# One stationary operand for both heads of a pair in the first score pass, and a prologue in another order

## The chip, the cores and the metric

The kernel runs on one core of a Trainium2 chip. Times are device microseconds of one execution; the profile is of one execution, taken by the hardware profiler. The engines are TensorE (PE in the rows; PEld is its weight load), VectorE (DVE), ScalarE (ACT), GpSimd (POOL) and SyncE (SP), which issues most DMA transfers. Each runs its own instructions in order and waits on semaphores.

## The reference

One layer of a language model tower on 32 sequences of 512 tokens, D = 256, all in float32. Cut to what matters:

```python
h = (tok_table[x] + pos_table + seg_table[seg]) * sqrt(256)      # seg: a running maximum over x == 102
xn = layernorm(h)
Q, K, V = heads(xn @ wq), heads(xn @ wk), heads(xn @ wv)         # 16 heads of 16
sc = einsum('bhnid,bhnjd->bhnij', Qb, Kw) / 4                    # a block of 64 queries, 128 keys: its own block and the one before
local = softmax(where(mask, sc, -inf)) @ Vw
GQ = heads(xn @ wgq)                                             # 8 latent heads of 16
GK, GV = heads(chunk_means(xn @ wgk)), heads(chunk_means(xn @ wgv))   # 64 latents
rem = softmax(where(lmask, GQ @ GK.T / 4, -inf)) @ GV @ r_out_w
h = h + (sigmoid(gate_l(Q)) * local + sigmoid(gate_r(Q)) * rem) @ w_out
h = h + ffn(layernorm(h))      # 8 experts, each takes the 2048 tokens that score best for it
```

## The kernel before

The program has a prologue, a loop over 32 sequences (written out, not a loop on the chip), and the experts. In the loop a sequence has five score passes, s = 0 to 4: s = 0 the latents, s = 1 to 4 the four tiles of 128 queries. A softmax needs the maximum of each row before its exponential, so every pass is made twice. The first pass (`top_scores`) puts queries on the partitions of the four PSUM banks `banks`; VectorE takes row maxima (`dve_tops`, L1160, into `mx`, or `mxl` for the latents). TensorE transposes these (task `MX`, L781), ScalarE negates and copies them (`low`, `lowl`), and SP writes them as extra rows into the query tiles by DMA (`Qt<-low` L467, `Gq<-lowl` L463). The second pass (`key_scores`) puts keys on the partitions and streams the queries: the extra row of Q times a row of ones in K takes the maximum off, and ScalarE's exponential (L686) follows. `values` (L1059, L1065) multiplies the probabilities with V. The second pass of u = s - 1 follows the first pass of s, and `half(2s)` stands between them.

Heads lie in pairs: 32 partitions (a strip, g = 0 to 3) hold two heads of 16. Two copies of each tensor exist, j = 0 and 1: `Qt[par][:, j, ...]` and `Kt[par][:, j, ...]` hold head j of the pair, with zeros in the other head's 16 rows, but for the row 16 * (1 - j) of each strip: it is the extra row of Q, and ones in K. ScalarE writes copies, zeros and ones in one go out of PSUM, by a scale per partition (`c_query`, `c_parity`) and a bias per partition (`c_unit`). In the first pass Q's extra row is still zero. Each score matmul uses one 32x64 tile of the array; eight tiles (four strips, two halves a) can be at work at a time. A float32 matmul is two records in the trace, so L1003 has 32 matmuls and 64 records in a pass. Ahead of them 16 bf16 records (L995) add the mask.

`plan` is a table written by hand: ten halves of tasks per sequence (projections Q, K, G, PK, PV, V and transposes ET for the next sequence; RT, RO, MT, WO for the output of a tile). Each engine walks through it in the same order. SP's `store` walks through it too: the rows of maxima after MX, and after WO the finished tile to `h_rows` (L474), which waits for GpSimd's factors (`s_fac`).

The prologue loads all weights and tables (SP, L449; everything waits for `s_load`, all 20 loads), turns token ids into rows of indices (VectorE L1332 to L1338, TensorE's transposes L928 and L930, `idx_now` L1129), gathers embedding rows (GpSimd L510), adds position and segment (VectorE `dve_embed`, L1136 on), normalises (GpSimd `pool_norm`, L517 to L525) and projects the first sequence (`head_tasks`, L776 on, Q at L802).

Of the kernel before, what the change touches and what calls it, by code (L numbers as in the profile page):

```python
# [26 lines left out]
P = 128  # L27
D = 256
# [30 lines left out]
def constants(S):  # L59
# [6 lines left out]
    unit = np.stack([i % 32 == HD, i % 32 == 0], 1)  # L66
# [19 lines left out]
    cols = [f(ident), f(parity * HD ** -0.5), f(parity), f(parity * (NL / S)), f(unit), f(before), f(lane), f(i),  # L86
# [6 lines left out]
def tower(nc, ins, out, cin, din, widths, SEQS, S, V, F, E):  # L93
# [12 lines left out]
    with ctx:  # L106
# [23 lines left out]
        (c_ident, c_query, c_parity, c_latent, c_unit, c_before, c_lane, c_part, onehot, ownhot, by_query, even_key, odd_key,  # L130
# [108 lines left out]
        r2 = sba("r2", [P, H, HD])  # L239
        mix = sba("mix", [P, D])  # L240
# [16 lines left out]

        s_load = sem("s_load")
# [166 lines left out]
        LOADS = 20  # L425
# [4 lines left out]
        def _(sp):  # L430
# [3 lines left out]
                (xi[:, :], ins["x"]), (cst[:, :], cin), (digits[:, :, :].rearrange("p a b -> p (a b)"), din),  # L434
                (b1_rows[:, :], ins["b1"].rearrange("e (m p) -> (e m) p", p=P)),
                (segs[:, 0, :], ins["seg_table"][0:1, :].to_broadcast([P, D])),
                (segs[:, 1, :], ins["seg_table"][1:2, :].to_broadcast([P, D])),
                (P16[:, :, :], ins["pos_table"].rearrange("(t p) d -> p t d", p=P)),
                (wq[:, :, :], v2(ins["wq"])), (wk[:, :, :], v2(ins["wk"])),
                (wvg[:, :, 0:D], v2(ins["wv"])), (wgq[:, :, :], v2(ins["wgq"])),  # L440
                (wgk[:, :, :], v2(ins["wgk"])), (wgv[:, :, :], v2(ins["wgv"])),
                (wro[:, :], ins["r_out_w"]), (wout[:, :, 0:D], v2(ins["w_out"])),
                (gates[:, 0, :], ins["gate_local_w"].rearrange("(a h) d -> a (h d)", a=1).to_broadcast([P, D])),
                (gates[:, 1, :], ins["gate_remote_w"].rearrange("(a h) d -> a (h d)", a=1).to_broadcast([P, D])),
                (cen[:, :], ins["centroids"]),
                (ln_rows[0:KC, :], v1(ins["ln_g"])), (ln_rows[KC:2 * KC, :], v1(ins["ln_b"])),
# [143 lines left out]
        def _(pool):  # L590
# [42 lines left out]
        def act_misc(act, m, task, b, nx):  # L633
# [20 lines left out]
            elif name == "Q":  # L654

                for j in range(2):
                    ins_ = nc.scalar.activation(Qt[nx][:, j, t, :], bank[:, :], ACT.Copy, scale=c_query[:, j:j + 1])
                ins_.then_inc(s_mA, 1)
            elif name == "K":

                for j in range(2):
                    ins_ = nc.scalar.activation(Kt[nx][:, j, t, W:], bank[:, :], ACT.Identity,
                                                scale=c_parity[:, j:j + 1], bias=c_unit[:, j:j + 1])
                ins_.then_inc(s_mA, 1)
            elif name == "G":
                for j in range(2):
                    ins_ = nc.scalar.activation(Gq[nx][:, j, :], bank[:, :], ACT.Copy, scale=c_query[:, j:j + 1])
                ins_.then_inc(s_mA, 1)
            elif name == "PK":
                for j in range(2):  # L670
                    ins_ = nc.scalar.activation(Gk[nx][:, j, :], bank[:, 0:NL], ACT.Identity,
                                                scale=c_latent[:, j:j + 1], bias=c_unit[:, j:j + 1])
# [56 lines left out]
        def _(act):  # L729

            act.wait_ge(s_init, 3)
# [191 lines left out]
        def _(pe):  # L923
            pe.wait_ge(s_load, 16 * LOADS)
            pe.wait_ge(s_init, 3)

            for t in range(TS):
                nc.tensor.transpose(M_ps[0][:, t * SEQS:(t + 1) * SEQS], xw[:, t * P:(t + 1) * P],  # L928
                                    c_ident[0:SEQS, 0:SEQS])
                nc.tensor.transpose(M_ps[0][:, (TS + t) * SEQS:(TS + t + 1) * SEQS], xs[:, t * P:(t + 1) * P],  # L930
                                    c_ident[0:SEQS, 0:SEQS])
            for c in range(KC):
                mm = nc.tensor.transpose(M_ps[1][:, c * E:(c + 1) * E], cen[:, c * P:(c + 1) * P], c_ident[0:E, 0:E])
# [545 lines left out]
```

## Time and profile before

| | |
|---|---|
| three runs | 2906.99, 2922.24, 2924.91 us; median 2922.24 |
| the profiled execution | 2924.72 us; its span 2922.7 us |
| busy in the span | PE 2667.8 us (91%), DVE 1737.8 (59%), ACT 1233.5 (42%), POOL 967.7 (33%) |
| TensorE's mean granted clock | 0.963 |

The span is what the profiler saw from the first to the last instruction; the 2 us to the time of the execution lie around it. A share of busy time is a mean over three stages of different kind, so the rows further down are read by stage.

### The profile page before, as it was taken

To read this page: it belongs to the slowest core of one execution; us is meant where nothing else is said; L and a number is where in the kernel's file an instruction comes from. 1 tells how busy PE (TensorE), PEld (TensorE's weight loads), DVE (VectorE), ACT (ScalarE), POOL (GpSimd) and SP (SyncE) were. 2 spreads that over 40 slices of the span, in tenths; PEclk is the share of its full clock that TensorE was granted. 3 is DMA by queue.
4 is the path that set the end of the run, shared out by engine and by line. 5 is a ranking of instruction groups with operands and counts; after the bars stand their busy time and mean duration, and the time that the engine had idled before them with its cause. 6 is when DMAs were issued, how large, how long until landed. Compare 5 with 4: busy or idle time off the path is not lost. (4 is left out here: it accounts for less than half of the span.)

```text
span 2922.7 us, 109244 instructions
## 1 busy us (share of the span) xinstructions
PE 2667.8 (91%) x47656; PEld 1862.1 (64%) x47656; DVE 1737.8 (59%) x5573; ACT 1233.5 (42%) x2659; POOL 967.7 (33%) x1417
## 2 busy tenths in 40 slices
PE   2799999999999999999999997169999999999998
PEld 1566677767767767677676676136666666666665
DVE  3466666666656666566665654766667575675700
ACT  0444444544444445454444542034434334344342
POOL 2323323323323324233233220024353443434433
PEclk9899999999999999999999998579999999999999
DMA  2000001000000000000000000101121112211120
GB/s 65 19 22 24 24 22 26 25 24 23 24 24 23 24 24 26 22 24 24 23 26 22 24 19 14 35 26 40 57 69 32 66 32 69 66 37 64 33 69 28
DMA packets 58915, 98.31 MB, mean 34 GB/s; under 512 B 12124, under 2 KB 43816, under 8 KB 58440
## 3 DMA queue, kind: packets, MB, share of 16 engines
q0 software_dynamic: 18624, 51.14, 6.2%
q1 hardware_dynamic: 39816, 40.17, 4.2%
q8 instruction: 378, 6.19, 0.9%
q14 instruction: 97, 0.79, 0.1%
HBM read 55.88 MB, written 33.82 MB: 31 GB/s over the span
## 5 line engine op out<-in xcount | busy, mean ns | idle before, releaser
L895 PE MATMUL banks<-hT,w 128*128 128x512 f32 x1024 | 468.6, 605 | 11.0 <-ACT hT L712 10.9
L1160 DVE TENSOR_REDUCE mx<-banks 128x8 f32<-128x1024 f32 x256 | 301.3, 1219 | 150.5 <-PE banks L1003 150.5
L686 ACT ACTIVATE probT<-banks 128x1024 f32<-128x1024 f32 x256 | 259.8, 1028 | 231.9 <-PE banks L1046 231.9
L723 ACT ACTIVATE hid<-banks,b 128x512 f32<-128x512 f32 x256 | 176.3, 689 | 399.0 <-PE banks L895 399.0
L532 POOL TENSOR_TENSOR h<-ve,mhalf 128x2 f32<-128x2 f32 x128 | 92.0, 719 | 737.1 <-DVE ve L1201 737.1
L895 PEld LDWEIGHTS banks<-hT,w 128*128 128x128 f32 x1024 | 187.6, 192 | 213.0 <-issue 197.3
L510 POOL DMA_INDIRECT rows<-in_tok_table,idx_now x132 | 138.5, 1049 | 475.3 <-DVE hres L1138 390.1
L1059 PEld LDWEIGHTS V_ps<-Ve,probT 128*64 128x64 f32 x4096 | 257.7, 141 | 34.4 <-issue 34.2
L1059 PE MATMUL V_ps<-Ve,probT 128*64 128x17 f32 x4096 | 271.4, 213 | 4.9 <-issue 4.9
L1059 PE MATMUL V_ps<-Vo,probT 128*64 128x17 f32 x4096 | 271.8, 213 | 2.2 <-issue 2.2
L1235 DVE TENSOR_SCALAR_CACHE_REDUCE hits<-act_s,cval 128x128 bf16<-128x128 f32 x960 | 261.2, 343 | 2.3
L1059 PEld LDWEIGHTS V_ps<-Vo,probT 128*64 128x64 f32 x4096 | 257.8, 141 | 4.1 <-issue 4.0
L575 POOL TENSOR_TENSOR orow<-orow,b 128x256 f32<-128x256 f32 x128 | 133.5, 1043 | 368.6 <-DVE orow L1325 367.5
L908 PE MATMUL M_ps<-w,hid 128*128 128x256 f32 x1024 | 231.6, 379 | 0.0
L908 PE MATMUL V_ps<-w,hid 128*128 128x256 f32 x1024 | 231.5, 379 | 0.0
L908 PEld LDWEIGHTS V_ps<-w,hid 128*128 128x128 f32 x1024 | 192.7, 190 | 38.9 <-issue 15.3
L908 PEld LDWEIGHTS M_ps<-w,hid 128*128 128x128 f32 x1024 | 190.3, 190 | 23.6
L1040 PE MATMUL banks<-Qt,Kt 32*64 32x128 f32 x4096 | 190.3, 284 | 3.1 <-issue 3.1
L1181 DVE TENSOR_TENSOR r<-M_ps,sg 128x256 f32<-128x256 f32 x128 | 54.4, 425 | 231.4 <-PE M_ps L787 230.3
L1040 PEld LDWEIGHTS banks<-Qt,Kt 32*64 32x64 f32 x4096 | 166.4, 132 | 23.0 <-issue 4.0
L1046 PE MATMUL banks<-Qt,Kt 32*64 32x64 f32 x4096 | 173.9, 225 | 7.5 <-issue 7.4
L1042 PE MATMUL banks<-Qt,Kt 32*64 32x64 f32 x4096 | 178.0, 228 | 0.5 <-issue 0.5
(223 smaller groups left out, 5566.2 us busy)
## 6 DMA issues: line engine op xcount, KB each, us to landing
h_rows<-h SPq DMA_DIRECT2D x128, 130.0 KB, 2.0
w<-in_w SPq DMA_DIRECT2D x16, 1024.0 KB, 5.3
Qt<-low SPq DMA_DIRECT2D x512, 2.0 KB
Gq<-lowl SPq DMA_DIRECT2D x256, 2.0 KB
rows<-in_tok_table,idx_now POOLq DMA_INDIRECT x132, 3.5
out_rows<-orow,idx_cur POOLq DMA_INDIRECT x128, 2.5
b<-in_b SPq DMA_DIRECT2D x8, 128.0 KB, 4.5
hrow<-h_rows,idx_next POOLq DMA_INDIRECT x64, 2.8
```

The lines of the kernel that those rows point to most:

```text
L510: nc.gpsimd.indirect_dma_start(rows[:, t, :], None, ins["tok_table"], bass.IndirectOffsetOnAxis(idx_now[:, t:t + 1], 0)).then_inc(s_rows[t ...
L575: nc.gpsimd.tensor_tensor(out=orow[:, q % 2, :], in0=orow[:, q % 2, :], in1=b2[:, :], op=ALU.add).then_inc(s_add, 1)
L686: nc.scalar.activation(dst[:, 2 * pair:2 * pair + 2, :], banks[:, 2 * pair:2 * pair + 2, :], ACT.Exp).then_inc(s_exp, 1)
L723: nc.scalar.activation(hid[:, m, :], S_ps[m % 2][:, 0:GT * P], ACT.Gelu_apprx_tanh, bias=b1[:, m:m + 1]).then_inc(s_hid, 1)
L895: mm = nc.tensor.matmul(S_ps[m % 2][:, 0:GT * P], w1[:, c, m * P:(m + 1) * P], hT[g % 2][:, c, :], start=c == 0, stop=c == KC - 1)
L908: mm = nc.tensor.matmul(O_ps[q % 2][:, 0:D], hid[:, m, q * P:(q + 1) * P], w2[:, m, :], start=m == 0, stop=m == FC - 1)
L1040: nc.tensor.matmul(banks[side[0], g, n * P:(n + 1) * P], k[:, W + at_:P + at_], q[:, at_:at_ + P], start=False, stop=n == G - 1)
L1042: nc.tensor.matmul(banks[side[1], g, n * P:n * P + W], k[:, at_:W + at_], q[:, at_:at_ + W], start=False, stop=False)
L1046: mm = nc.tensor.matmul(banks[side[1], g, n * P + W:(n + 1) * P], k[:, P + at_:P + W + at_], q[:, at_ + W:at_ + P], start=False, stop=n == ...
L1059: nc.tensor.matmul(V_ps[side[a], h * OW:(h + 1) * OW], probT[t % 2][:, g, n * P + a * W:n * P + (a + 1) * W], vals[:, t, h, :], start=True ...
L1160: nc.vector.tensor_reduce(tops.rearrange("p (g h) -> p g h", g=2), banks[:, 2 * pair:2 * pair + 2, :].rearrange("p g (h k) -> p g h k", h= ...
L1235: ins_ = nc.vector.tensor_scalar(hits[:, c, :], act_s[:, :], cval[:, c:c + 1].bitcast(F32), None, ALU.is_ge, ALU.add, accum_out=counts[:, ...
```

## The change

- First pass: ScalarE no longer zeroes the other head's rows of Q (the scale is a constant), only those of K, and writes no ones. One stationary tile, `Qt[par][strip, 0, ...]`, now serves both heads: the moving operand is `Kt[par][strip, :, ...]`, both copies j side by side, 2 x 128 columns (latents: 2 x 64), and the output goes to two places of the bank. There are half as many matmuls, each twice as wide. Masks, second pass and values stay.
- A row of ones in K would now spoil the first pass, since Q has the other head's values there. So K's row is zero in the first pass, and SP writes the ones from a constant tile `units` by DMA, after the first pass that last reads these columns (`s_S`) and before the second pass that needs them, which waits for them on `s_low[u]` together with the maxima.
- Prologue: ids and the identity are loaded first on semaphores of their own; the other loads stand in another order; VectorE starts on the ids alone, and the sums for the gates and some of the set-up stand later; TensorE makes the transposes of indices ahead of the wait for all loads; GpSimd normalises sequence 0 ahead of the gathers for sequence 1, and sequence 1 ahead of those for 2.

```diff
--- before.py
+++ after.py
@@ block.sync @@
-                (xi[:, :], ins["x"]), (cst[:, :], cin), (digits[:, :, :].rearrange("p a b -> p (a b)"), din),
...
+                (cst[:, P:], cin[:, P:]), (digits[:, :, :].rearrange("p a b -> p (a b)"), din),
             ]
+            sp.dma_start(xi[:, :], ins["x"]).then_inc(s_x, 16)
+            sp.dma_start(cst[:, 0:P], cin[:, 0:P]).then_inc(s_ident, 16)
...
             def store(b, q):
                 m = Misc(b, q % 2)
-                for half in plan:
+                for n, half in enumerate(plan):
+                    if m.new and n % 2 == 0:
+                        scored = n // 2
+                        done = [0] if scored == 0 else [] if scored == 1 else [scored - 1, scored][:1 + (scored == NU - 1)]
+                        if done:
+
+                            sp.wait_ge(s_S, 2 * (NU * b + scored + 1))
+                        for u in done:
+                            for j in range(2):
+                                if u == 0:
+                                    sp.dma_start(Gk[q % 2][HD * (1 - j)::32, j, :], units[:, 0, 0:NL]).then_inc(s_low[u], 16)
+                                else:
+                                    sp.dma_start(Kt[q % 2][HD * (1 - j)::32, j, :, W + (u - 1) * P:W + u * P],
+                                                 units[:, :, :]).then_inc(s_low[u], 16)
...
@@ block.gpsimd @@
             for t in range(TS):
+                pool_norm(pool, 0, t, 0, None)
+            for t in range(TS):
                 pool_gather_rows(pool, 1, t)
             for t in range(TS):
-                pool_norm(pool, 0, t, 0, None)
+                pool_norm(pool, 1, t, 1, Misc("head"))
             for t in range(TS):
                 pool_gather_rows(pool, 2, t)
-            for t in range(TS):
-                pool_norm(pool, 1, t, 1, Misc("head"))
@@ act_misc @@
-                    ins_ = nc.scalar.activation(Qt[nx][:, j, t, :], bank[:, :], ACT.Copy, scale=c_query[:, j:j + 1])
+                    ins_ = nc.scalar.activation(Qt[nx][:, j, t, :], bank[:, :], ACT.Copy, scale=HD ** -0.5)
...
-                    ins_ = nc.scalar.activation(Kt[nx][:, j, t, W:], bank[:, :], ACT.Identity,
-                                                scale=c_parity[:, j:j + 1], bias=c_unit[:, j:j + 1])
+                    ins_ = nc.scalar.activation(Kt[nx][:, j, t, W:], bank[:, :], ACT.Copy, scale=c_parity[:, j:j + 1])
...
@@ block.tensor @@
+            pe.wait_ge(s_ident, 16)
+            pe.wait_ge(s_init, 1)
+            for t in range(TS):
+                nc.tensor.transpose(V_ps[:, t * SEQS:(t + 1) * SEQS], xw[:, t * P:(t + 1) * P],
+                                    c_ident[0:SEQS, 0:SEQS])
...
+            mm.then_inc(s_setT, 1)
+
             pe.wait_ge(s_load, 16 * LOADS)
...
@@ top_scores @@
-                    for n in range(2 * TS):
-                        j, t = divmod(n, TS)
+                    for t in range(TS):
...
-                                mm = nc.tensor.matmul(banks[side[a], g, n * NL:(n + 1) * NL],
-                                                      Gq[par][strip[g], j, at_:at_ + W], Gk[par][strip[g], j, :],
-                                                      start=False, stop=n == 2 * TS - 1)
...
+                                mm = nc.tensor.matmul(
+                                    banks[side[a], g, :].rearrange("p (j t n) -> p j t n", j=2, t=TS)[:, :, t, :],
+                                    Gq[par][strip[g], 0, at_:at_ + W], Gk[par][strip[g], :, :],
+                                    start=False, stop=t == TS - 1)
...
-                for n in range(G):
-                    j, c = divmod(n, KC)
+                for c in range(KC):
...
-                            mm = nc.tensor.matmul(banks[side[a], g, n * P:(n + 1) * P],
-                                                  Qt[par][strip[g], j, c, at_:at_ + W],
-                                                  Kt[par][strip[g], j, c, at_:at_ + P], start=False, stop=n == G - 1)
...
+                            mm = nc.tensor.matmul(
+                                banks[side[a], g, :].rearrange("p (j c k) -> p j c k", j=2, c=KC)[:, :, c, :],
+                                Qt[par][strip[g], 0, c, at_:at_ + W],
+                                Kt[par][strip[g], :, c, at_:at_ + P], start=False, stop=c == KC - 1)
@@ key_scores @@
-                pe.wait_ge(s_low[u], (16 * 2 * (TS if u == 0 else KC)) * (b + 1))
+                pe.wait_ge(s_low[u], 16 * 2 * (1 + (TS if u == 0 else KC)) * (b + 1))
@@ block.vector @@
-            dve.wait_ge(s_load, 16 * LOADS)
+            dve.wait_ge(s_x, 16)
...
+            dve.wait_ge(s_setT, 1)
+            nc.vector.tensor_copy(idx_all[:, :, 0:SEQS], V_ps[:, 0:TS * SEQS].rearrange("p (t b) -> p t b", t=TS))
...
+            dve_indices(dve, 0)
...
+            dve.wait_ge(s_load, 16 * LOADS)
             chain(dve, nc.vector.tensor_tensor(P16[:, :, :], P16[:, :, :],
...
+            m = Misc("head")
+            dve_indices(dve, 1)
+            dve_embed(dve, 0, 0, 0, 0)
+            dve.wait_ge(s_setT, 2)
...
+            dve_latents(dve, m, 0)
+            dve_indices(dve, 2)
             for t in range(TS):
-                dve_embed(dve, 0, t, 0, 0)
...
+                dve_embed(dve, 1, t, 1, 0)
             for task in head_tasks:
                 dve_misc(dve, m, task, None, 1, 0)
-            for t in range(TS):
-                dve_embed(dve, 1, t, 1, 0)
```

On TensorE, in the first sequence, the latent pass and the first pass of tile 0, before:

```order
L976 MATMUL banks<-cst 64x512 x8
L985 MATMUL banks<-Gk,Gq 64x64 x64
L776 MATMUL M_ps<-cst,xn 128x128 x8
L781 MATMUL M_ps<-cst,mxl 32x128
L802 MATMUL M_ps<-x1T,wq 128x512 x2
L995 MATMUL banks<-cst 64x512 x16
L1003 MATMUL banks<-Kt,Qt 64x128 x32
L781 MATMUL M_ps<-cst,mx 16x128
```

And after:

```order
L996 MATMUL banks<-cst 64x512 x8
L1004 MATMUL banks<-Gk,Gq 64x2x64 x32
L792 MATMUL M_ps<-cst,xn 128x128 x8
L797 MATMUL M_ps<-cst,mxl 32x128
L818 MATMUL M_ps<-x1T,wq 128x512 x2
L1015 MATMUL banks<-cst 64x512 x16
L1022 MATMUL banks<-Kt,Qt 64x2x128 x16
L797 MATMUL M_ps<-cst,mx 16x128
```

Nothing moved here; the two groups of score matmuls have half the count and twice the columns.

On SP, one sequence of even number in the loop, from its latent maxima on (low0 and low1 hold the maxima of two tiles in turn), before:

```order
L463 DMA Gq0<-lowl 4x128 x8
L474 DMA h1_rows<-h1 128x260
L467 DMA Qt0<-low0 4x128 x4
L474 DMA h1_rows<-h1 128x260
L467 DMA Qt0<-low1 4x128 x4
L474 DMA h1_rows<-h1 128x260
L467 DMA Qt0<-low0 4x128 x4
L467 DMA Qt0<-low1 4x128 x4
L474 DMA h1_rows<-h1 128x260
```

And after:

```order
L469 DMA Gk0<-units 4x64 x2
L481 DMA Gq0<-lowl 4x128 x8
L492 DMA h1_rows<-h1 128x260
L485 DMA Qt0<-low0 4x128 x4
L492 DMA h1_rows<-h1 128x260
L471 DMA Kt0<-units 4x2x128 x2
L485 DMA Qt0<-low1 4x128 x4
L492 DMA h1_rows<-h1 128x260
L471 DMA Kt0<-units 4x2x128 x2
L485 DMA Qt0<-low0 4x128 x4
L471 DMA Kt0<-units 4x2x128 x4
L485 DMA Qt0<-low1 4x128 x4
```

The transfers of ones stand ahead of the maxima of s = 0, 2, 3 and 4, each group behind a wait for that first pass; the pair of u = 2 is the second `Kt0<-units` group.

On VectorE, in the prologue, the way from the ids to the first embedding, before (from the sum of position and segment on):

```order
L1352 TENSOR_TENSOR P<-P,segs 128x1024
...
L1363 MEMSET mx 128x32
L1365 CAST idx_all<-M_ps 128x4x32
L1368 CAST idx_all<-M_ps 128x4x3
L1369 MEMSET seg_all 128x4x3
...
L1129 COPY idx_now<-idx_all 128x4
L1396 TENSOR_TENSOR cenT<-cenT,banks 128x16
L1398 COPY gprod<-banks 128x2x256
```

And after:

```order
L1370 MEMSET seg_all 128x4x3
L1373 CAST idx_all<-V_ps 128x4x32
L1376 CAST idx_all<-V_ps 128x4x3
L1149 COPY idx_now<-idx_all 128x4
L1378 COPY seg_all<-V_ps 128x4x32
L1381 MEMSET Ve 128x1360
...
L1389 MEMSET h 128x2
L1392 TENSOR_TENSOR P<-P,segs 128x1024
```

The copy into `idx_now`, which lets GpSimd gather, stood behind the sums of tables and gates; now it stands ahead of them and of the large memsets.

## Rows read from the trace of the kernel before

**Rows 1.** Two stretches: PE, PEld, DVE, ACT, POOL busy us (instructions), granted clock, DMA.

```profile
0.00:96.56 96.56, 31.23 (x230) 18.81 (x230) 34.13 (x108) 16.76 (x42) 27.55 (x41) 0.95 0.20 55
96.56:1796.00 1699.44, 1637.34 (x42277) 1180.48 (x42277) 1043.09 (x2588) 804.25 (x1831) 537.34 (x976) 0.98 0.09 23
```

**Rows 2.** TensorE's waits from 96.56 to 1796 us: total us, times, longest.

```profile
PE banks L985 <- issue: 16.4, 12, 2.1
...
PE V_ps L1059 <- issue: 7.2, 12, 0.9
...
PE M_ps L791 <- issue: 3.5, 2, 1.9
```

**Rows 3.** The queue that brings instructions: packets, MB, share of 16 engines.

```profile
q8 instruction: 378, 6.19, 0.9%
```

**Rows 4.** TensorE's timeline at three score passes: start us, duration us, group.

```profile
910.08 1.15 PE L1003 MATMUL banks<-Kt,Qt 32*64 32x128 f32 x64
911.17 0.33 PE L791 MATMUL M_ps<-cst,mix 128*128 128x128 f32 x1
...
915.65 1.04 PE L1029 MATMUL banks<-Gq,Gk 32*64 32x512 f32 x16
916.62 0.33 PE L784 MATMUL M_ps<-cst,rem 128*128 128x128 f32 x1
...
951.10 1.54 PE L985 MATMUL banks<-Gk,Gq 32*64 32x64 f32 x128
952.57 0.44 PE L791 MATMUL M_ps<-cst,mix 128*128 128x128 f32 x2
```

**Rows 5.** Timelines of SP, VectorE and TensorE around the first pass of s = 3.

```profile
915.59 2.13 SPq L467 DMA_DIRECT2D Qt<-low  x4
...
927.62 0.32 SPq L474 DMA_DIRECT2D h_rows<-h  x1
...
931.81 2.36 DVE L1160 TENSOR_REDUCE mx<-banks 128x8 f32<-128x1024 f32 x2 [3.68 <-PE banks L1003]
...
934.51 0.65 PE L1023 MATMUL banks<-cst 32*64 32x512 bf16 x16
```

**Rows 6.** DMA issues: count, KB each, median us from issue to landing.

```profile
h_rows<-h SPq DMA_DIRECT2D x128, 130.0 KB, 2.0
...
rows<-in_tok_table,idx_now POOLq DMA_INDIRECT x132, 3.5
```

**Rows 7.** Timeline of the prologue and of the first sequence, several engines.

```profile
0.73 0.40 SPq L449 DMA_DIRECT2D xi<-in_x  x1
...
15.86 0.41 DVE L1332 CAST xf<-xi 32x512 f32<-32x512 int32 x1 [15.86 <-DMA ln_rows<-in_ln_b]
...
18.37 1.21 DVE L1338 TENSOR_TENSOR_SCAN xs<-xf 32x512 f32<-32x512 f32 x1
...
35.92 0.17 DVE L1129 COPY idx_now<-idx_all 128x4 int32<-128x4 int32 x1
...
45.02 0.17 DVE L1128 COPY seg_now<-seg_all 128x4 f32<-128x4 f32 x1 [6.46 <-DMA rows<-in_tok_table,idx_now]
...
53.97 0.60 POOL L517 TENSOR_TENSOR rs<-ve,mhalf 128x1 f32<-128x1 f32 x1
...
63.87 1.19 PE L802 MATMUL M_ps<-x1T,wq 128*128 128x512 f32 x1 [0.56 <-ACT x1T L643]
...
88.95 0.66 PE L776 MATMUL M_ps<-cst,xn 128*128 128x128 f32 x2 [5.87 <-POOL xn L525]
91.09 0.66 PE L776 MATMUL M_ps<-cst,xn 128*128 128x128 f32 x2 [1.48 <-POOL xn L525]
```

**Rows 8.** Two stretches around a stop, columns as in the first group.

```profile
897.00:899.20 2.20, 0.55 (x24) 0.41 (x8) 2.03 (x2) 0.14 (x2) 1.76 (x6) 1.00 0.01 3
899.30:902.60 3.30, 3.30 (x22) 2.27 (x22) 0.70 (x3) 1.14 (x3) 1.16 (x1) 0.50 0.10 35
```

**Rows 9.** SP's waits from 96.56 to 1796 us.

```profile
SPq L474 <- POOL h L543: 244.5, 93, 6.9
```

More of the change, by code:

```diff
@@ L256, in tower @@
         orow = sb("orow", [P, 2, D])
+        s_x = sem("s_x")
+        s_ident = sem("s_ident")
         s_load = sem("s_load")
@@ L938, in _ @@
             for c in range(KC):
-                mm = nc.tensor.matmul(M_ps[1][:, 64:64 + E], lnb_row[:, c, :], cenT[:, c, :],
+                mm = nc.tensor.matmul(T_ps[1][:, 0:E], lnb_row[:, c, :], cenT[:, c, :],
                                       start=c == 0, stop=c == KC - 1)
@@ L943, in _ @@
             for c in range(KC):
-                nc.tensor.matmul(banks[:, 1, 0:E], lnb_row[:, c, :], cenT[:, c, :], start=c == 0, stop=c == KC - 1)
-            for c in range(KC):
-                for k in range(KC):
-                    mm = nc.tensor.transpose(banks[:, 0, (c * KC + k) * P:(c * KC + k + 1) * P],
-                                             wout[:, k, c * P:(c + 1) * P], c_ident)
+                mm = nc.tensor.matmul(banks[:, 1, 0:E], lnb_row[:, c, :], cenT[:, c, :], start=c == 0, stop=c == KC - 1)
             mm.then_inc(s_setT, 1)
@@ L957, in _ @@
             for task in head_tasks:
+                if task == ("V", 0):
+                    pe.wait_ge(s_setE, 8)
                 pe_misc(pe, m, task, None)
-            pe.wait_ge(s_setE, 8)
             strip = [slice(32 * g, 32 * (g + 1)) for g in range(G)]
@@ L997, in top_scores @@
                                              .to_broadcast([32, G, P]), start=r == 0, stop=False)
-                for n in range(G):
-                    j, c = divmod(n, KC)
+                for c in range(KC):
                     for g in range(G):
@@ L1346, in _ @@
                 nc.vector.memset(Vo[par][:, :, :, HD:OW], 1.0)
+            for j in range(2):
+                nc.vector.memset(eps[:, 0, j:j + 1], (1.0 + EPS, 1.0)[j])
+                nc.vector.memset(eps[:, 1, j:j + 1], (EPS * EPS, EPS)[j])
+            nc.vector.memset(seg_all[:, :, SEQS:SEQS + AHEAD], 0.0)
+            dve.wait_ge(s_setT, 1)
+            nc.vector.tensor_copy(idx_all[:, :, 0:SEQS], V_ps[:, 0:TS * SEQS].rearrange("p (t b) -> p t b", t=TS))
+            numbers = V_ps[:, 0:TS * SEQS].rearrange("p (t b) -> p t b", t=TS)[:, :, 0:1]
+            chain(dve, nc.vector.tensor_copy(idx_all[:, :, SEQS:SEQS + AHEAD], numbers.to_broadcast([P, TS, AHEAD])))
+            dve_indices(dve, 0)
+            nc.vector.tensor_copy(seg_all[:, :, 0:SEQS],
+                                  V_ps[:, TS * SEQS:2 * TS * SEQS].rearrange("p (t b) -> p t b", t=TS))
+            for par in range(2):
                 chain(dve, nc.vector.memset(Ve[par][:, :, :, :], 0.0))
@@ L1367, in _ @@
-            numbers = M_ps[0][:, 0:TS * SEQS].rearrange("p (t b) -> p t b", t=TS)[:, :, 0:1]
-            nc.vector.tensor_copy(idx_all[:, :, SEQS:SEQS + AHEAD], numbers.to_broadcast([P, TS, AHEAD]))
-            nc.vector.memset(seg_all[:, :, SEQS:SEQS + AHEAD], 0.0)
-            nc.vector.tensor_copy(seg_all[:, :, 0:SEQS],
-                                  M_ps[0][:, TS * SEQS:2 * TS * SEQS].rearrange("p (t b) -> p t b", t=TS))
-            for c in range(KC):
-                nc.vector.tensor_copy(lnb_row[:, c, :], M_ps[1][:, 32 + KC + c:33 + KC + c].to_broadcast([P, P]))
@@ L1384, in _ @@
-            dve.wait_ge(s_setE, 4)
-            nc.vector.memset(st0[:, :], 0.0).then_inc(s_O, 1)
-            nc.vector.memset(st1[:, :], 0.0).then_inc(s_h1out[0], 16)
-            for j in range(2):
-                nc.vector.memset(eps[:, 0, j:j + 1], (1.0 + EPS, 1.0)[j])
-                chain(dve, nc.vector.memset(eps[:, 1, j:j + 1], (EPS * EPS, EPS)[j]))
-            nc.vector.memset(mv1[:, :, :], 0.0).then_inc(s_h1out[1], 16)
-            m = Misc("head")
-            dve_indices(dve, 0)
```

106 lines of the change are left out of this document (56 added, 50 removed).

## The prediction

> **What bounds the kernel now.** I read the table of stretches first [rows 1]. From 96.56 to 1796 us (31.6 of the 32 sequences of the attention loop) TensorE is busy 1637 of 1699 us, 96%; VectorE has 1043 us there, ScalarE 804, GpSimd 537. So in the loop a microsecond taken off TensorE's row of work is a microsecond of the kernel, as long as no other chain takes over. The stretch ahead of it is another matter: 96.56 us with TensorE busy for 31. There a chain of loads, VectorE and GpSimd sets the time. The third stage, the experts, isn't touched.
>
> Second, the table of TensorE's waits in the loop [rows 2]. Its largest entries are marked "issue": the engine waited for nothing that the profile shows, 16.4 us ahead of L985 alone, 7.2 ahead of L1059 and 3.5 ahead of L791, which follows L985. All stops of this kind in the loop sum to 41 us. I counted TensorE's instructions between the stops: the distances are multiples of 256, and its instructions arrive in transfers of 6.19 MB / 378 = 16.4 KB [rows 3]. I read a stop as the engine using up one such piece before the next has come; L985 has the most instructions per microsecond of the program.
>
> Third, the timeline of TensorE around the three kinds of score pass [rows 4]. This is the view on which the size of the main term rests. Each row's start, and the start of the row behind it, give the time that a group takes. L985 (128 matmul records, 64 columns each) takes 952.57 - 951.10 = 1.47 us. L1003 (64 records of 128 columns) takes 911.17 - 910.08 = 1.09. L1029 (16 records of 512 columns) takes 916.62 - 915.65 = 0.97. All three stream the same 8192 columns through the same 32x64 tiles. So the number of instructions costs time at 64 and 128 columns, and nearly none at 512.
>
> **Wide first pass.** The change halves L985 to 64 records of 128 columns, which is L1003's form: 1.47 - 1.09 = 0.38 us, 32 times, 12 us. It halves L1003 to 32 records of 256 columns. No row has that width. Its bounds are 0 (it stays at 1.09) and, by the straight line from 64 records at 1.09 through 128 at 1.47 down to 32, 0.19 us a pass; L1029's 0.97 lies between and is a form bound by its columns, so I take 1.09 - 0.97 = 0.12 us, 128 times, 15 us (range 0 to 24). Nothing else in TensorE's row moves. The two tensors read (both heads of a pair from one slice) and the copies on ScalarE are as long as before or shorter; ScalarE is half idle.
>
> **Fewer stops.** The loop has 2737 TensorE instructions a sequence and will have 384 fewer. L985 keeps 64 records and loads in 1.09 us instead of 128 in 1.47, and the pass ahead of L1059 thins out too. The stops ahead of L985, L1059 and L791 are 27 us [rows 2]; those inside the second pass (L1040 to L1046, 11 us) stay. I take 15 of the 27, since where a piece ends is luck. A stop costs twice: in the stretch 897.0 to 899.2 us TensorE is busy for 0.55 us of 2.2, and the next, 899.3 to 902.6, shows a granted clock of 0.50, the 1.2 GHz level [rows 8]. The loop's mean clock of 0.98 [rows 1] means about 4% of 1699 us at half rate, 68 us, so some 34 us lost; with over half of the stops gone I take 10 us back. Stops and clock together 25 us, with bounds from -5 (new stops elsewhere) to 27 + 27 = 54 if all that follow from L985, L1059 and L791 go.
>
> The Trainium skill speaks against this term: "Runtime: NRT & Kernel Launch", section "Instruction fetch mechanics", says that the sequencer fetches the next block of 256 instructions while it runs the current one and that crossing a block is mostly hidden. The trace agrees with the 256 and not with the hiding (16.4 us ahead of one line); by the page this term would be 0.
>
> **The ones by DMA.** Per sequence SP issues 10 more small transfers: two for the latents, two each for u = 1, 2, 3, 4, with a wait on the end of a first pass ahead of them. Three pairs have little time: those of u = 1, 2, 3 must land between the end of the next first pass and the second pass of u. The tightest is u = 2. VectorE sees the pass done at 931.81, and the second pass starts at 934.51 [rows 5]: 2.70 us. SP's issue of such rows takes 2.13 / 4 = 0.53 us each [rows 5]. How long a 4 KB transfer takes to land no row shows; a 130 KB store takes 2.0 us from issue to landing, a gathered tile 3.5 [rows 6]. With 2.0 the second one lands 0.53 + 2.0 = 2.53 us after the release: hidden by 0.2 us, and a transfer this small is nearer to the store. So the price is 0; with 3.5 it is 4.03 - 2.70 = 1.33 us, 32 times, 43 us. Behind the waiting SP stand the rows of maxima of the next MX task and one h_rows store. The new wait ends before the MX result exists (VectorE needs the same event and 2.36 us on top), so these are delayed by at most one pair's issue, 1.1 us, ahead of uses a whole pass later: 0.
>
> The skill's "DMA: Bandwidth & Descriptors", section "Anatomy of one DMA", puts a fixed cost of about 2.0 us on a transfer. Counted from the end of SP's issue that estimate would land the ones at 3.1 us, 0.4 late, and give 2844 us in place of my sum.
>
> **Prologue.** Before, VectorE starts at 15.86, released by the last of 20 loads; the ids were first, issued at 0.73 [rows 7]. After, it waits for the ids alone: 0.73 + 2.0 = 2.7 us with the store's landing time. The row copy of indices stood at 35.92. Ahead of it stay six id operations (15.86 to 19.58, 3.7 us), TensorE's eight transposes and short memsets, about 2.3 us more: indices at about 8.7. From indices to gathered rows took 45.02 - 35.92 = 9.1: rows at 17.8. The weight loads, which ended at 15.8, now share the queues with 512 KB of gathers, so I put them at 18, and position and segment sums (2.8 us) behind them: first embedding at 21 instead of 45.3. From here, before, GpSimd's normalisation began at 53.97, after four embeddings and four gathers for the next sequence, and Q followed at 63.87, 18.9 us after the rows. After, the first normalisation follows the first embedding; VectorE sets the pace: four embeddings at 1.95 and 2.3 us of set-up work put between them, 10.1, then 2.1 for the last normalisation and 1.2 to Q: Q at 34.4. That is 29.4 us earlier. Then in the first sequence TensorE stood 5.87 us ahead of its transposes and 1.48 ahead of each of three more [rows 7]: 10.3 us. After, GpSimd normalises sequence 1 ahead of the third gather, the second sequence's rows are there by about 42 and its last normalisation ends near 52, about when the latent pass does: all of it goes, and 0.6 is lost where V3 waits for VectorE's PV copy. Sum 29.4 + 10.3 = 39.7, taken as 40 us. Bounds: 27, if gathers and loads slow each other so that the first embedding waits until 34, and 44.
>
> **The sum.** 2924.7 (the profiled execution; the three runs go from 2907 to 2925, median 2922) - 40 - 12 - 15 - 25 = 2832; shifted by the 2.5 us between profile and median, 2830 us. What is late next: in the prologue VectorE's embeddings; in the loop TensorE still.
>
> **The rivals.** (a) The wide pass doesn't do what it says: 256 columns cost 1.09, since the same columns stream. The step from 64 to 128 to 512 columns in [rows 4] speaks against it. 2830 + 15 = 2845. (b) By the skill's page, fewer instructions bring no stop back: 2830 + 25 = 2855. (c) All stops that hang on the dense passes go: 2830 - 29 = 2801. (d) The ones land late by a gathered tile's time: 2830 + 43 = 2873. (e) Slower than before: SP is one queue in order, and the ones stand behind an h_rows store that waits for GpSimd's factors. Such a store waited up to 6.9 us [rows 9]. If it held SP into the tight pass by that much, the ones of u = 2 would come 6.9 - 0.2 = 6.7 us late, 32 times, 214 us: 3044. It decides from 92 / 32 = 2.9 us a sequence. Against it: the store ahead of that place was issued at 927.62, 4.2 us before the release at 931.81 [rows 5].
>
> **How the numbers follow.** Forecast 2830 with its own spread (prologue 27 to 44, pass 0 to 24, stops -5 to 54): 62%. (a) 9%, (b) 8%, (c) 10%, (d) 8%, (e) 3%. The range 2790 to 2872 takes in the forecast's bounds where not all fall on one side, (a), (b) and (c), and leaves out (d), (e) and the far tails. 1% of 2922, 29 us, is about what a measurement of this kernel can tell from no change, since its own runs spread over 18 us. Only (e) and the upper tail of (d) with a short prologue gain end above 2893: faster 0.93, same 0.04, slower 0.03.
>
> **What would show it.** First latent pass at about 55 instead of 81 us, minus what V3 waits; Q of the first sequence's loop at 56 instead of 96.56. L1003's successor 32 records in 0.97 us, L985's 64 in 1.09. In the waits, no "issue" ahead of the latent pass and the values; "DMA Kt" nowhere among TensorE's waits. The prediction is wrong if TensorE waits for the ones, if the wide matmuls take 1.09 us, or if the first gathers need far more than 9 us beside the loads.

## The result, and the profile after

The changed kernel takes 2781.26 us (median of four runs, 2778.41 to 2785.64) against 2914.61 (four runs, 2898.95 to 2924.91): the ratio is 0.9545, 95% interval 0.951 to 0.9581. The forecast was 2830 with a range from 2790 to 2872; the time lies 9 us below the range. The profiled execution took 2778.41 us (span 2776.6), 146 us less than that of before.

First the table of stretches, cut where Q of the loop's first sequence begins (56.6 us; before, 96.6). It answers to [rows 1].

```profile
0.00:56.46 56.46, 27.81 (x164) 17.65 (x165) 34.18 (x110) 14.90 (x41) 26.85 (x39) 1.00 0.31 86
56.46:1640.00 1583.54, 1563.75 (x35985) 1080.42 (x35985) 1036.64 (x2580) 770.89 (x1829) 536.56 (x975) 1.00 0.10 26
```

The prologue is 40 us shorter, with about the same busy times: waits have gone, not work. In the loop TensorE is busy 1563.75 of 1583.54 us, 98.7% in place of 96.3, and the granted clock is 1.00 in place of 0.98. From 96.56 to 1796 us the trace of before has 76 us at the 1.2 GHz level, this one none from 56.46 to 1640.

Second, TensorE's waits in the loop, as in [rows 2]. These are all entries marked "issue":

```profile
PE banks L1066 <- issue: 0.5, 1, 0.5
...
PE banks L1015 <- issue: 0.3, 1, 0.3
...
PE M_ps L818 <- issue: 0.2, 1, 0.2
```

41 us of stops have become 1. Not one stands ahead of the latent pass (L1004, which was L985), the values (L1079, L1059) or L807 (L791), and those inside the second pass (L1060 to L1066, which were L1040 to L1046) are gone but for 0.5. The queue that brings instructions, as in [rows 3], has 48 pieces less, 13%:

```profile
q8 instruction: 330, 5.41, 0.8%
```

Third, TensorE's timeline at the two first passes, as in [rows 4]: start, duration, group.

```profile
868.01 1.07 PE L1022 MATMUL banks<-Kt,Qt 32*64 32x256 f32 x32
869.01 0.44 PE L807 MATMUL M_ps<-cst,mix 128*128 128x128 f32 x2
...
907.69 1.15 PE L1004 MATMUL banks<-Gk,Gq 32*64 32x128 f32 x64
908.77 0.44 PE L807 MATMUL M_ps<-cst,mix 128*128 128x128 f32 x2
```

From start to start a tile's first pass takes 869.01 - 868.01 = 1.00 us (1.09 before) and the latents' 908.77 - 907.69 = 1.08 (1.47). Over all passes of the loop the median of a tile's is 0.974 against 1.084, so 0.11 us, 128 times: 14 us.

Fourth, VectorE, SP and TensorE around the first pass of s = 3, as in [rows 5]:

```profile
888.21 2.36 DVE L1180 TENSOR_REDUCE mx<-banks 128x8 f32<-128x1024 f32 x2 [2.13 <-PE banks L1022]
...
888.29 1.51 SPq L471 DMA_DIRECT2D Kt<-units  x2
...
891.07 0.65 PE L1043 MATMUL banks<-cst 32*64 32x512 bf16 x16
```

SP issues the ones 0.08 us after VectorE sees the pass done, so nothing held SP. The two issues take 1.51 us, and by the trace's semaphore events the second transfer is in at 890.93, 2.64 us after the first issue began and 0.14 us ahead of the second pass at 891.07. This is the tightest of the 32 sequences, and the only one whose issues take longer than 1.22 us; why is not known. The sequence before it is like the others:

```profile
837.52 2.36 DVE L1180 TENSOR_REDUCE mx<-banks 128x8 f32<-128x1024 f32 x2 [2.36 <-PE banks L1022]
...
837.61 1.17 SPq L471 DMA_DIRECT2D Kt<-units  x2
...
840.22 0.64 PE L1043 MATMUL banks<-cst 32*64 32x512 bf16 x16
```

The medians of the 32 are 1.17 us for the two issues, 2.29 us until the second transfer is in, and 0.32 us from there to the second pass. A pass that does wait for the ones starts 0.13 us after they are in (e8_halves, below). So the usual margin is 0.32 - 0.13 = 0.19 us, and in the tightest sequence it is used up: TensorE stood 0.09 us there. No wait on `Kt` is long enough to stand among TensorE's.

Last, the prologue, as in [rows 7]: the ids' release, the indices, the first gather, the first step that needs all loads, the first normalisation, the first Q, and Q in the loop's first sequence.

```profile
2.56 0.41 DVE L1352 CAST xf<-xi 32x512 f32<-32x512 int32 x1 [2.56 <-DMA xi<-in_x]
...
8.10 0.17 DVE L1149 COPY idx_now<-idx_all 128x4 int32<-128x4 int32 x1
...
9.23 1.10 POOL L528 DMA_INDIRECT rows<-in_tok_table,idx_now  x1 [8.40 <-DVE idx_now L1149]
...
19.57 1.23 DVE L1392 TENSOR_TENSOR P<-P,segs 128x1024 f32<-128x1024 f32 x1 [6.64 <-DMA digits<-in_digit_table]
...
24.74 0.58 POOL L535 TENSOR_TENSOR rs<-ve,mhalf 128x1 f32<-128x1 f32 x1 [10.64 <-DVE ve L1165]
...
36.34 4.61 PE L818 MATMUL M_ps<-x1T,wq 128*128 128x512 f32 x5 [0.56 <-ACT x1T L661]
...
56.61 1.96 PE L818 MATMUL M_ps<-x1T,wq 128*128 128x512 f32 x4
```

The last load now sets the start of the embeddings (VectorE stands 6.64 us for `digits`), no longer the row of indices.

So of the 146 us between the two profiles the prologue has 40, and the wide matmuls 12 and 14. The stops have 40. The stretches at half rate have 76 / 2 = 38; 65 of the 76 us begin within 3.5 us of the start of a stop, the others behind waits for other engines. That makes 144; 2 us aren't named. The prediction had 25 where the last two terms have 78. From the second latent pass to the last, 30 sequences that the prologue does not touch, the same terms can be set against a measured length: 1613 us before and 1522 after are 91 us, of which the streaming has 25, the stops 37 and the half rate 51 / 2 = 26.

### The profile page after: what moved, and what is told of

Read it like the earlier page. It is cut to its first block and busy times, and to the rows that moved or that the text cites. A ratio compares the mean times of both kernels' runs of the same rounds, so it can differ in the third digit from the quotient of the medians.

```text
span 2776.6 us, 97280 instructions
## 1 busy us (share of the span) xinstructions
PE 2597.7 (94%) x41512; PEld 1766.3 (64%) x41512; DVE 1737.3 (63%) x5575; ACT 1199.2 (43%) x2659; POOL 966.5 (35%) x1417
## 5 line engine op out<-in xcount | busy, mean ns | idle before, releaser
L1079 PEld LDWEIGHTS V_ps<-Ve,probT 128*64 128x64 f32 x4096 | 251.6, 139 | 34.6 <-issue 34.6
L1079 PE MATMUL V_ps<-Ve,probT 128*64 128x17 f32 x4096 | 264.4, 212 | 0.1
L1079 PE MATMUL V_ps<-Vo,probT 128*64 128x17 f32 x4096 | 264.4, 212 | 0.0
L1079 PEld LDWEIGHTS V_ps<-Vo,probT 128*64 128x64 f32 x4096 | 251.6, 139 | 0.0
L1060 PE MATMUL banks<-Qt,Kt 32*64 32x128 f32 x4096 | 186.9, 282 | 0.1
L1060 PEld LDWEIGHTS banks<-Qt,Kt 32*64 32x64 f32 x4096 | 165.1, 131 | 20.4 <-issue 0.4
L1062 PE MATMUL banks<-Qt,Kt 32*64 32x64 f32 x4096 | 175.2, 227 | 0.0
L597 POOL DMA_INDIRECT out_rows<-orow,idx_cur x128 | 137.1, 1071 | 109.5 <-POOL orow L593 90.9
```

Source lines behind the costliest of these rows:

```text
L597: nc.gpsimd.indirect_dma_start(out, bass.IndirectOffsetOnAxis(idx_cur[:, g * GT + q:g * GT + q + 1], 0), orow[:, q % 2, :], None).then_inc ...
L1060: nc.tensor.matmul(banks[side[0], g, n * P:(n + 1) * P], k[:, W + at_:P + at_], q[:, at_:at_ + P], start=False, stop=n == G - 1)
L1062: nc.tensor.matmul(banks[side[1], g, n * P:n * P + W], k[:, at_:W + at_], q[:, at_:at_ + W], start=False, stop=False)
L1079: nc.tensor.matmul(V_ps[side[a], h * OW:(h + 1) * OW], probT[t % 2][:, g, n * P + a * W:n * P + (a + 1) * W], vals[:, t, h, :], start=True ...
```

## The experiments

Three theories on those 78 us. A: the stop is local; it comes where 256 instructions are worked off faster than the next 256 arrive, and the clock falls behind it. B: the number of instructions of a sequence decides. C: the new prologue shifted the places at which pieces end. In the table, "stops" is the sum of the waits marked issue from 100 to 1640 us and "half rate" the time at 1.2 GHz from 57 to 1640 us by the trace's clock records; TensorE's instructions are matmuls, weight loads and a few for semaphores. The window is the same for all, so the slower kernels have fewer sequences in it. In before and e1_wide 14 us of the half rate are the stretch from 86.8 to 100.5 us, which begins while TensorE waits for `xn` in the old prologue [rows 7]. In the eleven traces 210 of the 211 stops from 60 to 1796 us stand at the same place of a piece of 256, counted from TensorE's first instruction on.

| kernel | median us (its before) | 95% interval of the ratio | instr. a sequence | stops us | half rate us |
|---|---|---|---|---|---|
| before | 2914.61 | 1 | 2737 | 38.8 | 68 |
| changed | 2781.26 (2914.61) | 0.951 to 0.9581 | 2353 | 1.0 | 0 |
| e1_wide | 2823.99 (2919.58) | 0.9645 to 0.9737 | 2353 | 1.7 | 14 |
| e2_prologue | 2878.49 (2919.58) | 0.9828 to 0.994 | 2737 | 37.6 | 55 |
| e3_latents | 2817.26 (2919.58) | 0.9621 to 0.9712 | 2609 | 18.9 | 14 |
| e4_tiles | 2840.0 (2919.58) | 0.9688 to 0.9793 | 2481 | 18.7 | 27 |
| e5_narrow | 2871.72 (2916.82) | 0.976 to 0.9903 | 2737 | 35.0 | 55 |
| e6_sparse | 2980.89 (2916.82) | 1.017 to 1.025 | 2665 | 1.5 | 14 |
| e7_dense | 2891.82 (2916.82) | 0.9874 to 0.9957 | 2609 | 24.2 | 7 |
| e8_halves | 2839.03 (2916.82) | 0.969 to 0.976 | 2353 | 4.9 | 27 |

**The two halves of the change.** e1_wide has the wide passes and the ones by DMA with the old prologue; e2_prologue has the new prologue with the old passes and data. Each is one half of the diff above and has no further edit.

> The wide first passes and the ones by DMA with the old prologue. Three theories on why TensorE's stops marked issue (41 us in the loop before, 1 us after) went. A: a stop comes where the program issues a piece of 256 instructions faster than the next arrives, so the stops went with the dense first passes. B: the loop's total number of instructions decides. C: the new prologue shifted the places where pieces end. A and B: hardly a stop in the loop, granted clock of the loop 1.00, sequences of 50.7 us, total near 2815 us. C: stops and the loop's clock of 0.98 stay as before, and only the streaming gain shows: near 2890 us.

> The new prologue with the old narrow passes. A and B: the first latent pass starts at about 53 us, the first sequence ends its wait chain as in the changed kernel, the loop keeps some 40 us of stops and a clock of 0.98; 28 us by the start of the loop and 10 to 18 us in the first sequence: 2870 to 2877 us. C: the stops go here too, about 2805 us.

The prologue alone gives 2919.58 - 2878.49 = 41 us (17 to 50 by the interval), the term of the prediction. The wide passes alone give 2919.58 - 2823.99 = 96, of which the prediction's three terms had 52. The two add up to 137, against 133 together. e1_wide has lost the stops with the old prologue, and e2_prologue keeps them with the new one: C falls. From the second latent pass to the last e1_wide takes 1522 us, as long as the changed kernel. Its time is 9 us above the 2815 that A expected.

**Latents wide alone, tiles wide alone.** Each is the changed kernel with one kind of first pass narrow again, its data and its ones as before (e3_latents shown; e4_tiles has the same edit at the latent pass).

```diff
@@ top_scores, e3_latents @@
-                for c in range(KC):
+                for n in range(G):
+                    j, c = divmod(n, KC)
...
-                                Qt[par][strip[g], 0, c, at_:at_ + W],
-                                Kt[par][strip[g], :, c, at_:at_ + P], start=False, stop=c == KC - 1)
+                                                  Qt[par][strip[g], j, c, at_:at_ + W],
+                                                  Kt[par][strip[g], j, c, at_:at_ + P], start=False, stop=n == G - 1)
```

> The changed kernel with the wide first pass and the ones for the latents alone; tiles stay narrow, as before (128 of the 384 instructions a sequence taken away). A: no stop ahead of the latent pass and the task behind it; those ahead of the values and inside the second passes stay at 15 to 20 us; about 2828 us. B: every place loses about a third of its stops, the latent pass keeps 10 us; about 2840 us.

> The changed kernel with the wide first pass and the ones for the tiles alone; latents stay narrow (256 of the 384 instructions taken away). A: the stops ahead of the latent pass stay (some 16 us, and the half-rate stretches behind them), those ahead of the values go; about 2845 us. B: two thirds of all stops go, of the latent pass's too; about 2815 us.

TensorE's waits marked issue with the latents wide alone (L1062 to L1068 is the second pass, L1081 the values):

```profile
PE V_ps L1081 <- issue: 5.1, 9, 0.9
...
PE banks L1068 <- issue: 4.8, 3, 1.9
...
PE banks L1062 <- issue: 2.9, 2, 1.6
...
PE banks L1064 <- issue: 2.1, 2, 1.6
```

and with the tiles wide alone (L1007 is the latent pass, L809 the group behind it, L1068 the second pass):

```profile
PE banks L1007 <- issue: 13.6, 7, 2.1
...
PE M_ps L809 <- issue: 3.5, 2, 2.0
...
PE banks L1068 <- issue: 1.4, 2, 1.2
```

e3_latents takes 2817.26 us (11 less than A expected) and e4_tiles 2840.0 (5 less). The two lists hardly overlap. The narrow latent pass makes the stops ahead of itself and behind itself; the narrow passes of the tiles make those ahead of the values and inside the second pass, 9.8 us there against 1.4. e4_tiles has fewer instructions than e3_latents (2481 against 2609), the same sum of stops, and is 23 us slower. By B it should have fewer stops and be the faster one. 13 us more at half rate are 7 of the 23; the rest is not explained.

**Narrow passes on the new data.** e5_narrow is the changed kernel with both first passes narrow and the ones still by DMA; the narrow form is that of the diffs above.

> The changed kernel with the score matmuls of the first passes narrow again (one for each head), on its data and with the ones by DMA. A (a stop comes where 256 instructions are issued faster than the next 256 arrive): the kernel with the prologue alone, 2878 us (2868 to 2890), again some 40 us of stops with L1004's and the values' successors at the head, sequences at 53.9 us, half-rate stretches of some 58 us. Rival F (part of the gain came from the lighter copies on ScalarE, or part was lost to the ones): the time differs from 2878 by over 12 us, and down to 2781 if the copies did it all.

e5_narrow takes 2871.72 us, 7 less than e2_prologue, and the runs overlap (2846 to 2884, 2873 to 2892): stops and half rate are back as well. So what the change does to ScalarE's copies and to SP's queue neither gains nor costs anything that shows; with runs 38 us apart, an effect of some 20 us would not show. e5_narrow and the changed kernel differ in the width of the matmuls alone, so the 90 us between their medians are that. From the second latent pass to the last the traces differ by 83 us; streaming makes 25 of it, stops 34, the clock 55 / 2 = 27: 86.

**More instructions, thin or dense.** e6_sparse cuts the projections into quarters, where 256 instructions take long; e7_dense cuts the longest matmuls of the second pass into halves.

```diff
@@ pe_misc, e6_sparse (V and WO likewise) @@
-                for c in range(KC):
-                    mm = nc.tensor.matmul(bank[:, :], w[:, c, t * P:(t + 1) * P], x1T[:, c, :],
-                                          start=c == 0, stop=c == KC - 1)
+                for i in range(4):
+                    for c in range(KC):
+                        mm = nc.tensor.matmul(bank[:, i * P:(i + 1) * P], w[:, c, t * P:(t + 1) * P],
+                                              x1T[:, c, i * P:(i + 1) * P], start=c == 0, stop=c == KC - 1)
@@ key_scores, e7_dense @@
-                        nc.tensor.matmul(banks[side[0], g, n * P:(n + 1) * P], k[:, W + at_:P + at_], q[:, at_:at_ + P],
-                                         start=False, stop=n == G - 1)
+                        for i in range(2):
+                            nc.tensor.matmul(banks[side[0], g, n * P + i * W:n * P + (i + 1) * W], k[:, W + at_:P + at_],
+                                             q[:, at_ + i * W:at_ + (i + 1) * W], start=False, stop=n == G - 1 and i == 1)
```

> The changed kernel with the projections Q, K, G, V and WO cut into four matmuls of a quarter of the columns: some 312 TensorE instructions a sequence more, 2665 in place of 2353, all in places where 256 instructions take long. A: no stop comes back (under 5 us marked issue in the loop, clock 1.00), and the time grows only by the shorter matmuls themselves, estimated at 31 x 26 x 0.1 to 0.6 us, so 2860 to 3260. B (the number of instructions of a sequence decides): some 30 us of stops and some 50 us of half-rate stretches, as at 2737 instructions.

> The changed kernel with the 128-column matmuls of the second pass (L1060) cut into two of 64: 256 instructions a sequence more, 2609 as with the narrow tile passes, all in the second pass; first passes stay wide. A: stops come back inside the second passes and at the values behind them, 8 to 20 us, half-rate stretches of 10 to 30 us, and 32 records more a pass cost about 0.19 us x 124 = 24 us: 2820 (2808 to 2845). D (only the first passes are dense enough, and the stops inside the second pass were theirs): under 3 us of stops, clock 1.00, 2805.

e6_sparse, waits marked issue, all of them from 100 to 1640 us:

```profile
PE M_ps L800 <- issue: 1.0, 1, 1.0
...
PE V_ps L1085 <- issue: 0.5, 2, 0.3
```

e7_dense, the largest of the same list (L1061 to L1067 is the second pass):

```profile
PE banks L1061 <- issue: 9.4, 11, 1.4
...
PE banks L1067 <- issue: 7.4, 9, 1.2
...
PE banks L1063 <- issue: 4.9, 6, 1.2
```

312 instructions more in thin places bring hardly a stop (1.5 us); 256 more in a dense place bring 24 us, nearly all inside the second pass, with both first passes wide. B falls, and so does D: the second pass can make stops by itself. A is left, with what stays open below. The 2980.89 us of e6_sparse are the price of short matmuls, which A allowed for; its 14 us at half rate A had not expected. They are two stretches, each 1.3 to 1.7 us behind the start of one of the two short stops at L1085. Here is the first stop, and the stretch after it with columns as in [rows 1]:

```profile
286.93 0.18 PE L1085 MATMUL V_ps<-Vo,probT 128*64 128x17 f32 x1 [0.28 <-issue]
...
288.30:295.10 6.80, 6.80 (x53) 4.45 (x53) 3.78 (x12) 0.82 (x2) 1.39 (x4) 0.50 0.01 1
```

In e7_dense I had the size wrong: 2891.82 in place of 2820. The second pass takes 2.44 us in place of 1.88 where no stop falls into it (medians of 89 and 123 passes from 57 to 1640 us, from the start of L1043 to the next group), so 0.56 us more and not the 0.19 taken from the step between 64 and 128 records [rows 4]. 124 x 0.56 = 69 us, stops 24, half rate 3: 96 of the 111 us.

**The margin of the ones.** e8_halves writes the same ones in four transfers of 2 KB.

```diff
@@ block.sync @@
-                                    sp.dma_start(Kt[q % 2][HD * (1 - j)::32, j, :, W + (u - 1) * P:W + u * P],
-                                                 units[:, :, :]).then_inc(s_low[u], 16)
+                                    for c in range(KC):
+                                        sp.dma_start(Kt[q % 2][HD * (1 - j)::32, j, c, W + (u - 1) * P:W + u * P],
+                                                     units[:, c, :]).then_inc(s_low[u], 16)
```

> The changed kernel with the ones of a tile written by four transfers of 2 KB in place of two of 4 KB. By the trace the second one landed 0.14 us ahead of its use at u = 2. If the margin is that thin: two more issues of 0.54 us each make the ones of u = 2 some 0.9 us late (0.7 to 1.4), 31 times, and TensorE shows waits on Kt there: 2810 (2800 to 2830). Rival: the issues overlap with the landing or the second pass waits for something else at that time anyway: 2781 to 2786, no such wait.

e8_halves takes 2839.03 us, 58 more than the changed kernel. First TensorE's waits in the whole loop, then the timeline at one u = 2, then two stretches around its start with columns as in [rows 1]:

```profile
PE banks L1044 <- DMA Kt<-units: 31.1, 58, 0.9
```

```profile
866.49 2.36 DVE L1181 TENSOR_REDUCE mx<-banks 128x8 f32<-128x1024 f32 x2 [2.36 <-PE banks L1023]
...
866.58 2.13 SPq L472 DMA_DIRECT2D Kt<-units  x4
...
869.88 1.08 PE L1044 MATMUL banks<-cst 32*64 32x512 bf16 x16 [0.62 <-DMA Kt<-units]
```

```profile
869.30:869.70 0.40, 0.00 (x0) 0.00 (x0) 0.36 (x3) 0.26 (x1) 0.00 (x0) 1.00 0.02 5
869.80:873.10 3.30, 3.22 (x111) 2.87 (x112) 1.97 (x6) 0.00 (x0) 1.20 (x2) 0.50 0.03 7
```

The margin is thin, as the trace of after says: 2.14 us of issues in place of 1.17 (medians of 32) is enough. The wait is 0.64 us on average at u = 2, and 0.35 at u = 3, which I had not counted. The clock pays again: of the seven half-rate stretches from 57 to 1640 us six begin during such a wait or at most 1.2 us after its start (the seventh behind a stop for instructions). 31 us of waits, 27 / 2 = 14 for the clock and 5 of stops make 50 of the 58. "The ones cost 0" held, by some 0.2 us.

**GpSimd's order in the prologue.** e9_gathers_first puts it back and keeps the early ids.

```diff
@@ block.gpsimd @@
+            for t in range(TS):
+                pool_gather_rows(pool, 1, t)
             for t in range(TS):
                 pool_norm(pool, 0, t, 0, None)
             for t in range(TS):
-                pool_gather_rows(pool, 1, t)
+                pool_gather_rows(pool, 2, t)
             for t in range(TS):
                 pool_norm(pool, 1, t, 1, Misc("head"))
-            for t in range(TS):
-                pool_gather_rows(pool, 2, t)
```

> The changed kernel with GpSimd's prologue in the order of before: gathers for sequence 1 ahead of the normalisation of sequence 0, those for sequence 2 ahead of that of 1. Local theory: the prologue's gain comes from two places, the early ids and this order. Q of sequence 0 comes 3 to 6 us later (four gathers issued ahead of the normalisation), and TensorE waits again for xn behind the first latent pass, up to 10 us: 2789 (2784 to 2797), first Q of the loop at 61 to 71 us instead of 56.6. Rival: the early ids alone did it, since four gathers are issued while the embeddings run: 2781, first Q of the loop at 57.

e9_gathers_first takes 2793.34 us (six runs, 2791.25 to 2796.91; the ratio to its before of 2922.6 us is 0.9553, 0.9516 to 0.9589), 12 us more than the changed kernel. These lines of its timeline are the last gather, the first normalisation, and Q twice:

```profile
31.95 0.94 POOL L528 DMA_INDIRECT rows<-in_tok_table,idx_now  x1 [1.38 <-DVE hres L1158]
...
33.02 0.83 POOL L535 TENSOR_TENSOR rs<-ve,mhalf 128x1 f32<-128x1 f32 x1
...
43.69 5.81 PE L818 MATMUL M_ps<-x1T,wq 128*128 128x512 f32 x8 [0.56 <-ACT x1T L661]
...
63.64 1.96 PE L818 MATMUL M_ps<-x1T,wq 128*128 128x512 f32 x4
```

GpSimd's normalisation stands behind four gathers that wait for the embeddings and starts at 33.02 in place of 24.74; Q follows at 43.69 in place of 36.34, and in the loop at 63.64 in place of 56.61. So 7 of the prologue's 40 us are this order, and 33 the early ids with the rest of the new order, which no run takes apart. The waits for `xn` behind the first latent pass, which I had expected to return, are 0.7 us. The other 5 us lie in the loop, where four stops for instructions (L1066, L830) take 4.9 us in place of 1. TensorE's instructions are the same in both kernels, so they alone do not settle where a stop comes.

## Why the prediction was wrong

**The step that failed** is the term "Fewer stops", 25 us. Stops and clock gave 78 by the profiles (40 + 38). The profiles differ by 146 us where the sum had 92; 53 of the 54 more are this term, 2 are not named, and the tiles gave 1 less. Three sentences of it failed.

- "I take 15 of the 27, since where a piece ends is luck." All 27 went. The end of a piece is luck, but whether it costs anything is not luck alone: it depends on how densely the instructions stand that are worked off meanwhile. In the trace of before (96.56 to 1796 us), the instructions of 8 pieces took under 2.7 us from first to last, and each of the 8 ended in a stop; in the changed kernel the shortest took 2.70. In e7_dense (57 to 1640 us) 20 took under 2.4, and 19 stopped. It is no sharp limit: a piece of 2.65 us in e6_sparse and one of 2.67 in e1_wide did not stop.
- "Those inside the second pass (L1040 to L1046, 11 us) stay." They went with the narrow passes of the tiles (e3_latents against e4_tiles), though the second pass itself is unchanged. I had put a stop down to the line at which it shows. A piece of 256 instructions spans more than one group, so the cause can stand ahead of it.
- "With over half of the stops gone I take 10 us back" for the clock. All of it came (34 by the prediction's estimate, 38 by the clock records), since next to nothing is left that lets TensorE stand in the loop.

The bounds of the term failed too: their upper end of 54 had no gain from the second pass's stops and 27 us of clock, for which it gives no row, and lies 24 us short.

**The Trainium skill's page**, "Runtime: NRT & Kernel Launch", section "Instruction fetch mechanics", which calls the crossing of a 256-instruction block mostly hidden, agrees with the changed kernel (1 us of stops on 286 pieces in the loop) and not with before or e7_dense (39 and 24 us). e6_sparse and e7_dense show that here it depends on how densely the instructions stand.

**What was right.** The prologue: 40.0 us by the first Q of the loop, 41 by e2_prologue, its two parts (Q of the prologue 63.87 to 36.34, and the rest up to the loop's Q) 27.5 and 12.5 rather than 29.4 and 10.3. The ids' release (2.56 us for 2.7), the indices (8.10 for 8.7) and Q (36.34 for 34.4) came as worked out; the late Q is the last load, at 19.6 in place of 18. The latents' pass: 1.08 us for 1.09. The tiles': 1.00 for 0.97, 14 us for 15. The ones: 0; their landing was estimated at 2.53 us and was 2.29 in the median of 32. The prediction's other estimate for them, 3.1 us (which makes 2843 us, not 2844), was too long: the second transfer is in 1.1 us after the end of its issue, not 2.0. The section that it was taken from (the Trainium skill, "DMA: Bandwidth & Descriptors", "Anatomy of one DMA") is on transfers that GpSimd issues; these were SP's.

**The rivals.** (a) falls by the 0.974 us of the wide pass. (b), no stop comes back, falls by 2781 against 2872 with narrow passes. (c) was the nearest at 2801: it had all stops that hang on the dense passes, but not those inside the second pass. (d), the ones late, did not come about, and e8_halves shows that 1.0 us of issue time more would have brought it, at 58 us. (e), SP held by a store, did not either: SP issued 0.08 us after the release.

**What stays open.** In all 43 stops of before (96.56 to 1796 us), work resumed 2.2 to 3.0 us after the transfer of the next piece had begun, but that transfer began anywhere from 0.6 to 5.6 us after the piece ahead of it, and no run tells what starts it. So a piece's length foretells the 8 stops behind pieces under 2.7 us, and not the 35 behind longer ones. That half-rate stretches follow idle time of TensorE is read from traces (before, e6_sparse, e8_halves); no experiment set an idle time by itself, and e7_dense, with 24 us of stops of 1.4 us at most, has only 7 us at half rate, against 27 in e4_tiles with 19 us of stops of up to 2.1.

## What to carry to other kernels

Where the waits show "issue" on a saturated TensorE, count its instructions between the stops, and look at how little time the densest 256 take, across group boundaries; fewer and wider matmuls there gave back three times what the streaming gave (78 against 26 us). Price such a stop with the time at half rate behind it, and do not leave it at the line at which it shows. A transfer that is hidden by some 0.2 us is at no cost and has next to no margin: two issues more cost 58 us. Read such a margin from all sequences: the one first looked at was the tightest of 32.

## What the hardware showed that I had not expected

- Idle times as short as 0.3 us (e6_sparse, 288.30 to 295.10 us) and 0.6 us (e8_halves, 869.80 to 873.10 us), in a loop where TensorE is otherwise busy, were followed by stretches at the 1.2 GHz level, whatever the engine had waited for. Most idle times were not: in e8_halves it was 6 of the 58 waits for the ones.
- SP's issue of the ones took 0.59 us a transfer of 4 KB (1.17 / 2) and 0.53 one of 2 KB (2.14 / 4, e8_halves), medians of 32, while a row of maxima took 0.53 [rows 5]: halving the size does not halve the issue.
- Cutting 16 matmuls of 128 columns into 32 of 64 (32 records more) cost 0.56 us in the second pass, where 64 records more had cost 0.38 in the first [rows 4].
